# Adding the shift of a LayerNorm on GpSimd per tile instead of per two-tile unit, in a three-layer graph network

## The reference, cut to what matters

```python
msg = h[src]
agg = segment_sum(msg, dst) / maximum(count, 1)
h = residual + agg @ Wl.T + bl + h @ Wr.T        # residual: 0 in layer 0, then the layer's own input
h = (h - mean(h)) * rsqrt(var(h) + 1e-5) * g + b  # LayerNorm; g multiplies, b is the shift
h = where(h >= 0, h, a * h)                       # PReLU
```

## Time and profile before

| | |
|---|---|
| median of three runs | 2143.94 us (2139.96 to 2144.84) |
| profiled execution, its own time | 2149.07 us |
| span of it, first to last instruction | 2147.3 us |
| mean granted TensorE clock | 0.987 of full speed |
| busy in the span | TensorE 2046.7 us (95%), VectorE 1692.0 (79%), GpSimd 1506.6 (70%), ScalarE 1226.3 (57%) |
| `add_shift`, L689 | 235 instructions, 605.9 us |
| chain that ended last | TensorE 46%, GpSimd 22%, VectorE 12%, issue 12%, ScalarE 7% |

### The profile page before, as it was taken

One profiled execution on the slowest core, in us unless ns is written; L12 is line 12 of the kernel. 1 busy time (PEld: TensorE's weight loads), 2 busy tenths in 40 slices (PEclk: granted clock), 3 DMA queues, 4 the chain that ended last, 5 costly groups with the idle time before them and its releaser, 6 DMA issues.

```text
span 2147.3 us, 30989 instructions
## 1 busy us (share of the span) xinstructions
PE 2046.7 (95%) x10302; PEld 1683.9 (78%) x10302; DVE 1692.0 (79%) x2605; ACT 1226.3 (57%) x2565; POOL 1506.6 (70%) x1196
## 2 busy tenths in 40 slices
PE   6998999999999999999999999999999999999993
PEld 4877777788888788888888888887778888878872
DVE  6869887878887688877777777789878888888883
ACT  4864544544444355444444444478877777777775
POOL 2887877788878555655555555478887788777775
PEclk8999999999999999999999999999999999999997
DMA  5656766666666545444444444456666555565551
GB/s 181 209 201 229 220 199 199 194 205 202 210 210 210 160 153 172 160 147 148 148 147 148 148 148 148 142 192 205 213 203 191 187 189 198 184 201 187 192 171 67
DMA packets 180942, 387.46 MB, mean 180 GB/s; under 512 B 20107, under 2 KB 20552, under 8 KB 180782
## 3 DMA queue, kind: packets, MB, share of 16 engines
q1 hardware_dynamic: 142222, 271.80, 38.8%
q0 software_dynamic: 38560, 113.67, 16.1%
HBM read 220.81 MB, written 164.79 MB: 180 GB/s over the span
## 4 chain that ended last, share of the span: by engine, by line
PE 46%; POOL 22%; DVE 12%; issue 12%; ACT 7%; POOLq 0%; DMA 0%; ACTq 0%; DVEq 0%; SPq 0%
PE ps_z L408 38%; POOL y L689 8%; PE ps_t L389 5%; DVE hout L826 4%; DVE y L813 4%; POOL rstd L681 3%; PE ps_s L401 3%; POOL hin L652 2%; POOL orstd L695 2%; POOL out L706 2%; ACT junk L524 2%; ACT stage L573 2%; ACT o_sb L587 2%; DVE o_sb L868 1%; POOL node_found L730 1%
## 5 line engine op out<-in xcount | busy, mean ns | idle before, releaser
L408 PE MATMUL ps_z<-w_hi,hT_hi 128*128 128x512 f32 x1884 | 760.6, 404 | 4.2 <-DVE y L813 4.2
L408 PE MATMUL ps_z<-w_hi,hT_lo 128*128 128x512 f32 x1884 | 746.4, 396 | 0.0
L408 PE MATMUL ps_z<-w_lo,hT_hi 128*128 128x512 f32 x1884 | 745.2, 396 | 0.0
L689 POOL TENSOR_TENSOR y<-y,shift 128x1024 f32<-128x1024 f32 x235 | 605.9, 2578 | 164.8 <-DVE y L813 155.7
L524 ACT ACTIVATE junk<-ps_z 128x512 f32<-128x512 f32 x471 | 279.4, 594 | 490.3 <-DVE ps_z L805 448.1
L795 DVE TENSOR_TENSOR hT_lo<-ps_t,hT_hi 128x1024 fp32r<-128x1024 f32 (+1 forms) x237 | 287.9, 1215 | 178.3 <-ACT hT_hi L512 165.4
L408 PEld LDWEIGHTS ps_z<-w_hi,hT_lo 128*128 128x128 f32 x1884 | 355.0, 188 | 86.0
L408 PEld LDWEIGHTS ps_z<-w_hi,hT_hi 128*128 128x128 f32 x1884 | 356.3, 189 | 78.9 <-DVE y L813 2.9
L408 PEld LDWEIGHTS ps_z<-w_lo,hT_hi 128*128 128x128 f32 x1884 | 355.8, 189 | 78.5
L681 POOL TENSOR_TENSOR rstd<-veps,minus_half 128x2 f32<-128x2 f32 (+1 forms) x237 | 229.5, 969 | 259.1 <-ACT veps L530 258.6
L826 DVE SCALAR_TENSOR_TENSOR hout<-hout,slope_less,y 128x1024 f32<-128x1024 f32 (+1 forms) x237 | 377.6, 1593 | 4.0 <-ACT hout L539 4.0
(11 more groups left out here) (134 smaller groups left out, 2219.4 us busy)
## 6 DMA issues: line engine op xcount, KB each, us to landing
h_scratch<-hout SPq DMA_DIRECT2D x156, 512.0 KB
hin<-h_scratch SPq DMA_DIRECT2D x156, 512.0 KB
x_by_slot<-hin SPq DMA_DIRECT2D x78, 512.0 KB
o_sb<-x_by_slot SPq DMA_DIRECT2D x78, 512.0 KB
rowtab<-edge_row_table SPq DMA_DIRECT2D x60, 256.0 KB
stage<-in_WrT SPq DMA_DIRECT2D x3, 1024.0 KB
stage<-in_WlT SPq DMA_DIRECT2D x3, 1024.0 KB
hin<-in_x,node_get POOLq DMA_INDIRECT x157
```

What stands on the lines that cost most here:

```text
L408: mm = pe.matmul(acc, a[:, k, :], ww[:, k, :], start=start, stop=stop and k == KC - 1 and a is a_lo)
L689: nc.gpsimd.tensor_tensor(y[u.r2][:, 0:u.n, :], y[u.r2][:, 0:u.n, :], moved, ALU.add).then_inc(shifted, 1)
```

## The change

`add_shift` no longer waits for both scaled tiles of the unit and then adds the shift to 128x1024 elements in one instruction; it goes tile by tile, waits for the scaled rows of that tile alone, and adds the shift to 128x512 elements. The semaphore `shifted`, which counted units, counts tiles, so its other users are adapted: `part` on ScalarE still waits for the whole unit, and `add_late_shift` on VectorE, still one instruction, adds the number of tiles to it.

```diff
             def part(u):
-                act.wait_ge(shifted, u.no + 1)
+                act.wait_ge(shifted, u.upto)
...
             def add_shift(u):
                 if u.no >= LATE:
                     return
-                pool.wait_ge(gained, u.upto)
-                moved = shift[:, u.l:u.l + 1, :].to_broadcast([P, u.n, D])
-                nc.gpsimd.tensor_tensor(y[u.r2][:, 0:u.n, :], y[u.r2][:, 0:u.n, :], moved, ALU.add).then_inc(shifted, 1)
+                moved = shift[:, u.l, :]
+                for j in range(u.n):
+                    pool.wait_ge(gained, u.ahead + j + 1)
+                    nc.gpsimd.tensor_tensor(y[u.r2][:, j, :], y[u.r2][:, j, :], moved, ALU.add).then_inc(shifted, 1)
...
                 dve.wait_ge(gained, u.upto)
-                dve.wait_ge(shifted, u.no)
+                dve.wait_ge(shifted, u.ahead)
                 moved = shift[:, u.l:u.l + 1, :].to_broadcast([P, u.n, D])
-                nc.vector.tensor_tensor(y[u.r2][:, 0:u.n, :], y[u.r2][:, 0:u.n, :], moved, ALU.add).then_inc(shifted, 1)
+                nc.vector.tensor_tensor(y[u.r2][:, 0:u.n, :], y[u.r2][:, 0:u.n, :], moved, ALU.add).then_inc(shifted, u.n)
```

## The result

The changed kernel took 2153.71 us (median of 8 runs, 2152.37 to 2155.59) against 2143.52 us for the kernel before on the same chip (8 runs, 2139.96 to 2148.38): a ratio of 1.0047, 95% interval 1.0035 to 1.0060, or 10.2 us more. A later comparison gave 1.0037 (1.0023 to 1.0051). The change makes the kernel slower, by little but measurably, and by more than the 3.6 us that were forecast.

The account below looks back on a forecast made before the run. The prediction took TensorE to bound layer 1 and GpSimd's unbroken chain the plain units of layers 0 and 2. Its terms, 1.7 - 1.8 + 1.0 + 2.4 + 0 + 0.3 = +3.6 us on 2143.94, gave 2147.5 us, range 2136 to 2157.

Parts of the forecast that it names:

- The price of the split, 0.15 us: Everywhere the add is cut: two adds cost GpSimd 0.15 us more than one, with bounds of 0 and 0.42.
- Layer 1, 0: Layer 1, where TensorE never stops: neither gains nor losses of GpSimd change the time, 0 us.
- Layer 0, plain, +1.7 and -1.8: Layer 0's plain beats: eleven periods pay 0.15 us; at 157 to 190 us VectorE gets through after the first half.
- Layer 0, edges, +1.0: Layer 0's edge units: seven beats where TensorE waits for a low part behind an add pay 0.15 us each.
- Layer 2, plain, +2.4: Layer 2's plain beats: nineteen adds pay 0.15 us each, +2.9, less 0.5 gained by one add that waits for VectorE.
- No L868 over 2 us: Sign to look for in layer 2: VectorE's L868, 3.12 us beside the uncut add, stays at or under 2 us.
- Layer 2, edge groups, 0 within -9 to +5: Layer 2's 16 edge groups: shifted waits leave the low part within 0.1 us of its place; 0, bounds -9 to +5.
- The tail, +0.3: End of the kernel: three adds on the way to the end cost +0.3 us.
- The third: Rival: GpSimd keeps the ports through both halves, so layer 0's -1.8 us is lost; 2149.3 us, chance 0.07.
- The second rival: Layer 2's plain beats: PReLU starts before GpSimd's scatter, which then takes 2.06 us; +8.8 us, 2156.3 us, chance 0.13.
- The first: Rival: VectorE gets in before the next add in layer 2, -8.5 us plain, -4 edge groups; 2135.0 us, chance 0.22.
- the fourth: Rival: the split costs nothing, so the +0.15 us of 37 adds falls away; 2141.9 us, chance 0.08.

Follow-up runs that it names:

- e4: The changed kernel with each tile's add cut again into two column halves, four adds per unit: 2208.80 us, ratio 1.0289 to the kernel before.
- e2: The changed kernel with the early start taken back, two adds per unit both waiting for both scaled tiles: 2172.73 us, ratio 1.0116 to the kernel before.
- e3: The changed kernel with the second add also waiting until the first is complete: 2171.49 us, ratio 1.0119 to the kernel before.
- e10: The kernel before with the add cut in two only in layer 0 from its first edge unit on: 2153.77 us, ratio 1.0027.
- e8: The changed kernel once more, unedited, for a second trace and ratio: 2153.28 us, ratio 1.0037 to the kernel before.
- e5: The kernel before with the add cut in two only in layer 0: 2155.79 us, ratio 1.0053.
- e6: The kernel before with the add cut in two only in layer 2 from its first edge unit on: 2140.09 us, ratio 0.9977.

## Why the forecast was right in its direction and short in its size

- **The price of the split, 0.15 us: right.** Two adds, four adds (e4) and the beats of layer 0 (7.90 against 7.77, both averaged over four beats) agree on 0.13 to 0.15. In layer 2's plain beats it was 0.11 (7.64 against 7.53).
- **Layer 1, 0: right.** 644.13 and 643.99 us cut; 643.8 to 644.4 in the traces where this layer is uncut.
- **Layer 0, plain, +1.7 and -1.8: the failed step.** It was "with the split VectorE gets through after the first half, 1.2 us earlier". It doesn't: a PReLU that a late add held is now held by both halves, 3.05 for 2.90, 3.83 for 3.70, and in layer 2's groups 4.15 where it was 3.89. The four beats from 152 to 187 us lost 0.7 us instead of gaining 1.8. The +1.7 came out as 1.2. And the sum had nothing for the beats ahead of them, which lost 1.8 us: the early start was counted as a gain wherever it occurs, and at 65 us it puts the pair in front of the splitting of the weights (e2). Together 4.0 us (159.2, the mean of the traces cut here, less 155.2, that of the uncut; e2, e3, e4 and e10 are left out) where the sum had -0.1.
- **Layer 0, edges, +1.0: mis-sized most.** 6.4 us (566.0 against 559.5 in the means of the traces without and with the one add; e2, e3 and e4, which cut otherwise, are left out). I had multiplied 0.15 us by seven waits. But the delays add up over beats in which GpSimd has no idle time, to 1.3 us near 400. TensorE's low clock after the long wait has its part in it, 1.0 us in the beat behind (9.02 us, the mean of four traces, against e2's 8.04).
- **Layer 2, plain, +2.4: sign right,** 1.3 us (145.8 against 144.5) up to the first edge unit, and 0.5 more in the three beats behind it, which the forecast counted here and the table counts with the edges: 1.8 us. "No L868 over 2 us" fails: it takes 3.33 where it took 3.12, held by both halves.
- **Layer 2, edge groups, 0 within -9 to +5: inside its bounds,** -5.1 (560.8 against 565.9, three cut and five uncut traces), -5.5 without the three beats above. The order of events was foreseen ("the second add then starts 0.16 earlier in front of L826 instead of behind it") but counted as worth nothing, as the relief of TensorE's waits was not followed to the end of the group. "The first L826 (3.89) gets done 1.2 us earlier" was wrong.
- **The tail, +0.3:** nothing (43.2 and 43.1 us behind the last transpose).
- **The rivals.** The third, no hand-over between the halves, was right about the mechanism where the pair stands straight behind another instruction of GpSimd, with the smallest chance, and too low in its time, 2149.3, as it took back only the -1.8. The evidence weighed against it, that a root behind an add always let VectorE in, was about another kind of successor. The second rival's mechanism exists (e3) and did not occur: the scatter stayed ahead of PReLU. The first did not occur: layer 2's plain beats got longer. The split isn't free: the fourth falls.
- **What was luck.** The forecast's own odds were 0.40 for no change that can be measured and 0.38 for slower, and its range of 2136 to 2157 us holds three of the four rivals' times as well. That 2153.71 lies in it says little. The sign came out of a sum in which a gain of 1.8 us that does not exist stood against two losses that were put 1.8 and 5.4 us too low.

The stretches sum up to 4.0 + 6.4 + 0.1 + 1.3 - 5.1 = 6.7 us. That is inside the interval of e8 (4.9 to 10.9 us) and 0.8 us under that of the first comparison (7.5 to 12.9), whose before had the lowest median of the four that were taken (2143.52, 2146.72, 2144.81, 2148.29); those 0.8 us are not accounted for. The whole kernels add up as well: e5 and e6 give 11.4 - 4.9 = 6.5, with layer 2's plain 1.3 us 7.8, against 7.9 for e8.

By the Trainium skill's page "SBUF — State Buffer", section "Who interferes with whom", whoever issues first keeps the shared ports for that instruction. The PReLU of 4.15 us, shown starting 0.52 us before the pair of adds that holds it, speaks against the first part, and its length against the second: here GpSimd keeps the ports over two instructions.

What stays open: which beats between 187 and 390 us let GpSimd fall behind was not tried one by one; nor why e10's plain stretch, which isn't cut, takes 157.34 us. Of its 2.1 us over before, 1.1 lie in the first four beats, which vary by up to 0.7 us among the uncut traces, and 1.0 in the last beat, next to the first cut unit. In that beat its granted clock was 0.50 from 180 to 184 us, where the kernel before had 1.00; but e6 had 0.57 there and lost nothing. Nor was it tried why a pair out of idle time lets VectorE in and another doesn't.

## What to carry to other kernels

Where two engines take turns at a shared resource, cutting an instruction in two does not by itself offer a turn: look in the trace whether the other engine's stretched instruction ends at the first part's end or at the last's, and whether the parts come out of idle time or follow other work. An earlier start takes the turn from the other engine. That pays where the engine that starts earlier is the one that is late (the third add of a group here) and costs where the other is (the splitting of the weights in layer 0), so count both and cut there alone where it pays, and let the rest keep one instruction. And a fixed price on an engine without idle time is not paid once for each wait downstream: it adds up until something else has slack.

## What the runs showed of the hardware

- Two adds of 128x512 elements, one behind the other without idle time: if GpSimd comes to the first straight from another instruction, VectorE's instruction with two SBUF inputs waits for both (PReLU 4.15 us for 1.28); if it comes to the first out of idle time, VectorE gets in between them (1.87, and the second add takes 2.31 instead of 1.29). In all traces but those of e3 and e4: 278 of 278 and 72 of 72. This is counted in the traces, and no edit tested it by itself. A wait for the first one's completion lets it in too (3.05, and the pair then takes 3.56 instead of 2.55). A root behind them lets it in and takes 1.71 for 0.71.
- Who holds the ports is not told by the start times shown. In the trace of before 43 adds came out of idle time while a PReLU or a splitting was running, begun 0.16 or 0.17 us earlier, and none held it. Of 49 that came straight behind another GpSimd instruction, 39 held theirs (a PReLU, a sum or a splitting, begun 0.08 to 0.69 us earlier) beyond their own end, and 10 did not (begun 0.74 to 0.95 earlier). The same in all traces but those of e3 and e4: 312 of 312 not held out of idle time (0.16 to 0.52), and behind another instruction 385 of 385 held up to 0.69 us, 109 of 109 not held from 0.74 on. e4, with its shorter adds, has three exceptions (0.06, 0.07 and 0.20 us, not held).
- An indirect DMA on GpSimd took 2.06 us for 1.04 when PReLU had started 0.11 us before it.
- The same beats of the same kernel took TensorE 33.6 us in one trace and 29.4 in another: in the first it stood idle for most of 290 to 294 us and its granted clock was then 0.50 from 294 to 298, in the second the clock stayed at 1.00. The kernel before itself spread over 2139.85 to 2149.65 us in 48 runs, on several chips.
